# A first stage by half batches: ScalarE normalises, the gates go round by DMA in four rows, and VectorE adds the residual's bias

## The chip, the cores and the metric

One core of a Trainium2 chip runs the kernel. The metric is the device time of one execution in microseconds, the lower the better; the median of three runs is compared.

## The reference

One transformer block with modulation (adaLN), in float32, on x of 4 batches x 1024 tokens x 256:

```
mod = (silu(c) @ wmod)                  # 4 rows x 1536: sa, ca, ga, sb, cb, gb
ga, gb = sign(g) * max(|g|, 0.25)       # each gate is kept away from 0
h = layernorm(x) * (1 + ca) + sa
x = x + ga * attention(h)               # 8 heads, low-rank q, k, v (32 + 32 rotary columns), softmax
h = layernorm(x) * (1 + cb) + sb
x = x + gb * moe(h)                     # top 1 of 8 experts, capacity 768, exact gelu
```

`attention` ends in `o @ W_O + b_O`; the kernel carries the value path as 32 latent columns per head, so that W_UV and W_O fold into one matrix `proj` (256 x 256) and the biases into one row `attn_bias`.

## The kernel before

Four stages follow each other, each a block in which every engine runs its own written-out list; semaphores order them. All engines leave a block together. Here only stage one and the head of stage two matter.

**Stage one** (lines 185 to 518) makes for each batch b of 8 tiles (128 tokens each): the moments of x (`spread(b)`, VectorE, L312 to L317), the power -1/2 of the variance (GpSimd, L299), the normalised rows `xn` (VectorE, L324), their transposes (`turn(b)`, TensorE, L428), the modulated transposes `hT` (`features(b)`, ScalarE, L255, scale and shift from the columns `shiftT`), and with them two latents in PSUM: `latent(b, 0)` for the keys and `latent(b, 1)` for the queries (L443). ScalarE writes their high half (KA L265, KC L266, CQ L268), VectorE the low half (L403, L406) and KB (L408); `values(b)` turns KA (L452), and VectorE copies it to VV (L412). `latent(b + 1, ...)` waits on `lo_done` until the low half of batch b has been taken out of the same PSUM bank. `xn` and `hT` hold one batch.

Beside this TensorE does 15 `side` products in the one bank `t_ps2`, each of which waits until VectorE has copied the one before (`side_out`): 0 and 1 turn W_UQ, 2 turns W_UK and W_UV, 3 multiplies them (VectorE makes G and GQ of that, L339 to L350), 4 and 5 make `proj`, 6 makes `attn_bias`, and 7 to 14 make the four gates of each batch, replicated on all 128 partitions: the weights of that product are `silrep`, silu(c) spread over 128 columns, two products of 512 columns per batch (L489). VectorE copies each (L357) and after the second bounds the gates in five steps (L363 to L369) on 128 partitions. The columns `shiftT` come before all that from eight small products with `wm` as weights (L501).

The SP queue loads in this order: rows, x of batch 0, the first third of wmod, the up-weights (16 loads), x of batch 1, W_O, b_O, the rest of wmod, x of batches 2 and 3, and then writes zeros to the DRAM buffer `xbuf`, 6.4 MB; SP waits for those before it leaves the block. GpSimd fills constants, among them two of 4096 columns at 3.5 us each (L293), before its first power.

**Stage two** (from L520) runs the 32 heads. GpSimd starts it with `prepare(b)` for each batch (L733 to L741): `projb` = proj x gate, `gbias` = attn_bias x gate, and x1 += gbias over the batch's 2048 columns (L740). After that it makes `prob_lo` for most tiles (L745), and later normalises heads. TensorE first does queries (L652) and maxima (L633, L634), which VectorE reduces (L774), and scores from then on. `projb` and x1 are read only in stage three.

Of the kernel before, what the change touches and what calls it, by code (L numbers as in the profile page):

```python
# [41 lines left out]
def adaln_block(nc, h_t, W_DQ, b_DQ, W_UQ, b_UQ, W_DKV, b_DKV, W_UK, b_UK, W_UV, b_UV, W_QR, b_QR,  # L42
# [16 lines left out]
    out_rows = out.rearrange("b s d -> (b s) d")  # L59

    ctx = ExitStack()
    with ctx:
# [51 lines left out]

        one = ExitStack()
        xs = x1
# [13 lines left out]
        silrep = sb(one, "silrep", [P, B, KD, P])  # L130
        bvrep = sb(one, "bvrep", [P, H, P])
        onesrow = sb(one, "onesrow", [1, P])
        shiftT = sb(one, "shiftT", [P, 4, B])
# [4 lines left out]
        stats = sb(one, "stats", [P, ST, 6])  # L138
        mv = sb(one, "mv", [P, ST, 2])
        vare = sb(one, "vare", [P, ST])  # L140
        rstd = sb(one, "rstd", [P, ST])
        xn = sb(one, "xn", [P, ST, D])
        hT = sb(one, "hT", [P, KD, S])
        sign = sb(one, "sign", [P, 2, D])
        size = sb(one, "size", [P, 2, D])
# [6 lines left out]
        x_in = [sem(f"x_in{b}") for b in range(B)]  # L152
        rows_in = sem("rows_in")
        shift_in = sem("shift_in")
        up_in = sem("up_in")
        latent_in = sem("latent_in")
        gates_in = sem("gates_in")
# [5 lines left out]
        shift_ready = sem("shift_ready")  # L163
# [4 lines left out]
        gate_steps = sem("gate_steps")  # L168
        ln_v = sem("ln_v")
        ln_var = sem("ln_var")  # L170
        ln_rstd = sem("ln_rstd")
        ln_xn = sem("ln_xn")
# [6 lines left out]
        v_done = sem("v_done")  # L179

        SIDE = 7 + 2 * B

        with nc.Block() as block:
            @block.sync
            def _(sp):
# [4 lines left out]
                def load_x(b):  # L192
                    load(xs[:, b * ST:(b + 1) * ST, :], x_tiles[:, b * ST:(b + 1) * ST, :], x_in[b])
# [4 lines left out]
                wm_k = wmod.rearrange("(k p) n -> p k n", p=P)  # L198
                load(wm[:, :, 0:2 * D], wm_k[:, :, 0:2 * D], shift_in)
# [23 lines left out]
            def _(ac):  # L223
# [20 lines left out]
                def features(b):  # L244

                    if b == 0:
                        ac.wait_ge(shift_done, 2)
                    else:

                        ac.wait_ge(kq_ready, 2 * b)  # L250
                    for g in range(2):
                        for k in range(KD):
                            n = 4 * b + 2 * g + k
                            ac.wait_ge(xT_ready, n + 1)
                            nc.scalar.activation(hT[:, k, g * HALF:(g + 1) * HALF], t_ps[n % 2][:],  # L255
                                                 ACT.Identity, scale=shiftT[:, 2 + k, b:b + 1],
                                                 bias=shiftT[:, k, b:b + 1]).then_inc(hT_ready, 1)

                features(0)
                for b in range(B):  # L260

                    if b == 0:
                        ac.wait_ge(latent_in, 16 * 14)
                    ac.wait_ge(kq_ready, 2 * b + 1)
                    nc.scalar.activation(KA[:, b * S:(b + 1) * S], k_ps[:], ACT.Identity, bias=bk[:]).then_inc(hi_done, 1)  # L265
                    nc.scalar.activation(KC[LR:P, b, :], k_ps[LR:P, HALF:S], ACT.Identity, bias=bk[LR:P, :]).then_inc(hi_done, 1)  # L266
                    ac.wait_ge(kq_ready, 2 * b + 2)
                    nc.scalar.activation(CQ[0:3 * DC, b * S:(b + 1) * S], q_ps[0:3 * DC, :], ACT.Identity,  # L268
                                         bias=bq[:]).then_inc(hi_done, 1)
                    if b + 1 < B:  # L270
                        features(b + 1)

            @block.gpsimd
            def _(pool):
# [5 lines left out]
                for m in (ident, ident16):  # L280
# [8 lines left out]
                fills = ((ones16[:], 1.0), (onesrow[:], 1.0), (VV[:, :, 2 * DC:VP], 1.0),  # L289
                         (KB[LR:LR + 1, :], -1.0), (CQ[3 * DC:QROWS, :], 1.0))  # L290
                for n, (dst, value) in enumerate(fills):
                    pool.wait_ge(const_p, 9 + n)
                    nc.gpsimd.memset(dst, value).then_inc(const_p, 1)  # L293
                pool.wait_ge(const_p, 14)
                pool.wait_ge(const_v, 2)
                for b in range(B):

                    pool.wait_ge(ln_var, b + 1)
                    nc.gpsimd.tensor_tensor(rstd[:], vare[:], minus_half[:], ALU.pow).then_inc(ln_rstd, 1)  # L299

            @block.vector
            def _(v):
                nc.vector.memset(zeros[:], 0.0).then_inc(const_v, 1)
                nc.vector.memset(minus_half[:], -0.5).then_inc(const_v, 1)
# [3 lines left out]
                def spread(b):  # L308

                    v.wait_ge(x_in[b], 16)  # L310
                    for t in range(ST):
                        nc.vector.bn_stats(stats[:, t, :], xs[:, b * ST + t, :]).then_inc(ln_v, 1)  # L312
                    v.wait_ge(ln_v, b * (2 * ST) + ST)
                    for t in range(ST):
                        nc.vector.bn_aggr(mv[:, t, :], stats[:, t, :]).then_inc(ln_v, 1)
                    v.wait_ge(ln_v, (b + 1) * (2 * ST))
                    nc.vector.tensor_scalar(vare[:], mv[:, :, 1], EPS, None, ALU.add).then_inc(ln_var, 1)  # L317

                def normalise(b):
                    v.wait_ge(ln_rstd, b + 1)  # L320
                    if b:
                        v.wait_ge(xT_ready, 4 * b)
                    for t in range(ST):
                        nc.vector.tensor_scalar(xn[:, t, :], xs[:, b * ST + t, :], mv[:, t, 0:1],  # L324
                                                rstd[:, t:t + 1], ALU.subtract, ALU.mult).then_inc(ln_xn, 1)

                def side_out(n):
# [3 lines left out]
                    if n < 2:  # L331
                        nc.vector.tensor_copy(uqT[:, 4 * n:4 * n + 4, 0:QROWS],
                                              bank[:].rearrange("p (h c) -> p h c", h=4)[:, :, 0:QROWS]).then_inc(side_done, 1)
                    elif n == 2:
                        nc.vector.tensor_copy(ukvT[:], bank[:].rearrange("p (h c) -> p h c", h=H)).then_inc(side_done, 1)
                    elif n == 3:

# [6 lines left out]
                        v.wait_ge(side_done, 4)  # L344
# [6 lines left out]
                    elif n < 6:  # L351
                        nc.vector.tensor_copy(proj[:, n - 4, :], bank[:, 0:D]).then_inc(side_done, 1)
                    elif n == 6:
                        nc.vector.tensor_copy(attn_bias[:], bank[:, 0:D]).then_inc(side_done, 1)
                    else:
                        b, half = (n - 7) // 2, (n - 7) % 2
                        nc.vector.tensor_copy(mod[:, b, 2 * half:2 * half + 2, :],  # L357
                                              bank[:].rearrange("p (m d) -> p m d", m=2)).then_inc(side_done, 1)
                        if half:

                            v.wait_ge(side_done, n + 1)
                            g = mod[:, b, 0:4:3, :]
                            nc.vector.tensor_scalar(sign[:], g, 0.0, 2.0, ALU.is_ge, ALU.mult).then_inc(gate_steps, 1)  # L363
                            nc.vector.scalar_tensor_tensor(size[:], g, -1.0, g, ALU.mult, ALU.max).then_inc(gate_steps, 1)
                            v.wait_ge(gate_steps, 5 * b + 2)
                            nc.vector.tensor_scalar(g, size[:], 0.25, None, ALU.max).then_inc(gate_steps, 1)
                            v.wait_ge(gate_steps, 5 * b + 3)
                            nc.vector.scalar_tensor_tensor(g, sign[:], -1.0, g, ALU.add, ALU.mult).then_inc(gate_steps, 1)
                            nc.vector.tensor_scalar(mod[:, b, CB, :], mod[:, b, CB, :], 1.0, None, ALU.add).then_inc(gate_steps, 1)  # L369
                            v.wait_ge(gate_steps, 5 * b + 5)  # L370
# [5 lines left out]
                normalise(0)  # L376
                v.wait_ge(shift_ready, 1)
                nc.vector.tensor_copy(shiftT[:, 0:2, :], t_ps[1][:, 0:2 * B].rearrange("p (m b) -> p m b", b=B)).then_inc(shift_done, 1)
                nc.vector.tensor_scalar(shiftT[:, 2:4, :], t_ps[1][:, 2 * B:4 * B].rearrange("p (m b) -> p m b", b=B),
                                        1.0, None, ALU.add).then_inc(shift_done, 1)  # L380
                v.wait_ge(cols_done, 1)
                nc.vector.tensor_copy(bvrep[:], cols[:, 88:96].unsqueeze(2).broadcast_to([P, H, P])).then_inc(cols_done, 1)
                v.wait_ge(silu_done, 1)
# [1079 lines left out]
```

## Time and profile before

| what | value |
|---|---|
| median of 3 runs | 1013.93 us (1011.23 to 1013.94) |
| profiled execution | 1015.22 us, its span 1013.5 us |
| mean granted clock of TensorE | 0.940 |
| TensorE busy | 902.4 us, 89% |
| VectorE busy | 719.9 us, 71% |
| GpSimd busy | 679.5 us, 67% |
| ScalarE busy | 573.6 us, 57% |

The span runs from the first to the last instruction; the rest of the execution's time lies around it. Busy time counts instructions in the engine and not waiting. A line number is that of the kernel's file; the order of engines' work is what the lists above say.

### The profile page before, as it was taken

How to read it: one execution, taken by the hardware profiler on the slowest of the kernel's cores; microseconds unless marked ns; L12 is line 12 of the kernel's file. 1: busy time of each engine (PE TensorE's matmuls, PEld its weight loads, DVE VectorE, ACT ScalarE, POOL GpSimd, SP SyncE). 2: the span in 40 equal slices, each digit the busy share in tenths (PEclk: the TensorE clock that was granted, in tenths of full speed). 3: DMA queues.
4: the chain of work that ended last, by engine and by line, in shares of the span. 5: the costliest groups of instructions: out<-in, count | busy, mean ns of one | idle time of the engine just before them, and what ended most of it. 6: DMA issues, size and time to landing. Idle time of an engine off the chain costs nothing. (4 is left out here: it accounts for less than half of the span.)

```text
span 1013.5 us, 21524 instructions
## 1 busy us (share of the span) xinstructions
PE 902.4 (89%) x8438; PEld 540.9 (53%) x8438; DVE 719.9 (71%) x1344; ACT 573.6 (57%) x972; POOL 679.5 (67%) x445
## 2 busy tenths in 40 slices
PE   4896799999999999999999998973399999999995
PEld 3442144444444444445444446863167776777764
DVE  5677878888888888888988854873065676566643
ACT  1222367777777777777677672655175447544650
POOL 4102989999999999999999993598505434543452
PEclk9899599999999999999999997985599999999998
DMA  9700000000000000000000002458715334544110
GB/s 274 295 0 1 1 1 2 2 1 2 2 2 1 3 1 3 2 2 2 2 1 3 1 2 98 153 188 284 251 48 180 124 119 135 181 128 132 46 50 19
DMA packets 48222, 69.50 MB, mean 69 GB/s; under 512 B 7440, under 2 KB 40405, under 8 KB 48122
## 3 DMA queue, kind: packets, MB, share of 16 engines
q1 hardware_dynamic: 38170, 51.01, 15.1%
q0 software_dynamic: 7680, 16.87, 5.1%
q8 instruction: 68, 1.11, 0.5%
q10 hardware_dynamic: 2272, 0.24, 0.2%
q14 instruction: 32, 0.26, 0.1%
HBM read 44.66 MB, written 29.66 MB: 73 GB/s over the span
## 5 line engine op out<-in xcount | busy, mean ns | idle before, releaser
L745 POOL TENSOR_TENSOR prob_lo<-prob 128x1024 f16<-128x1024 f32 x208 | 437.2, 2132 | 36.2 <-ACT prob L700 36.2
L700 ACT ACTIVATE prob<-st_ps 128x512 f32<-128x512 f32 x512 | 301.8, 597 | 134.8 <-PE st_ps L624 132.4
L774 DVE TENSOR_REDUCE part_max<-x_ps 128x1 f32<-128x512 f32 x512 | 325.1, 678 | 69.9 <-PE x_ps L634 68.9
L623 PE MATMUL st_ps<-QA,KA 128*128 128x512 f16 x512 | 199.3, 389 | 0.5 <-ACT prob L700 0.5
L624 PE MATMUL st_ps<-QB,KB 65*128 65x512 f16 x512 | 197.9, 387 | 0.0
L672 PE MATMUL acc_ps<-VV,prob 128*128 128x65 f16 x2048 | 159.6, 194 | 4.3 <-POOL prob_lo L745 4.3
L672 PEld LDWEIGHTS acc_ps<-VV,prob 128*128 128x128 bf16 x2048 | 143.9, 98 | 34.1 <-POOL prob_lo L745 6.8
L672 PE MATMUL acc_ps<-VV,prob_lo 128*128 128x65 f16 x2048 | 158.9, 194 | 0.0
L672 PEld LDWEIGHTS acc_ps<-VV,prob_lo 128*128 128x128 f16 x2048 | 135.2, 98 | 30.2 <-issue 0.5
L1255 POOL DMA_INDIRECT out<-yo,xb x48 | 47.7, 994 | 154.0 <-DVE yo L1362 149.1
L633 PE MATMUL x_ps<-KA,QA 64*128 64x512 f16 x256 | 102.9, 402 | 20.7 <-DVE part_max L774 20.7
L1285 ACT ACTIVATE act_f<-g_ps,cols 128x768 f32<-128x768 f32 x64 | 57.7, 901 | 105.0 <-PE g_ps L1408 98.2
L1333 DVE TENSOR_TENSOR act_l<-act_f,act_h 128x768 f16<-128x768 f32 x64 | 59.9, 956 | 72.7 <-ACT act_h L1293 71.7
L1423 PE MATMUL y_ps<-w2h,act_h 128*128 128x256 f16 x384 | 104.8, 273 | 4.2 <-DVE act_l L1333 4.2
L1423 PE MATMUL y_ps<-w2h,act_l 128*128 128x256 f16 x384 | 104.7, 273 | 0.0
L1423 PE MATMUL y_ps<-w2l,act_h 128*128 128x256 f16 x384 | 104.7, 273 | 0.0
L634 PE MATMUL x_ps<-KC,QA 64*128 64x512 f16 x256 | 102.8, 402 | 0.0
L633 PEld LDWEIGHTS x_ps<-KA,QA 64*128 64x128 f16 x256 | 23.8, 93 | 123.3 <-DVE part_max L774 120.2
L623 PEld LDWEIGHTS st_ps<-QA,KA 128*128 128x128 f16 x512 | 49.7, 97 | 60.4 <-issue 37.1
L1248 POOL DMA_INDIRECT tb<-tbuf,xb x48 | 63.9, 1332 | 17.0 <-issue 14.3
L791 DVE TENSOR_TENSOR prob_lo<-prob 128x1024 f16<-128x1024 f32 x48 | 61.1, 1274 | 6.2 <-ACT prob L700 6.2
L1408 PE MATMUL g_ps<-xh,w1h 128*128 128x384 f16 x256 | 53.4, 332 | 1.8 <-DVE xl L1327 1.4
(176 smaller groups left out, 1391.0 us busy)
## 6 DMA issues: line engine op xcount, KB each, us to landing
w1f<-in_L_ffn_w SPq DMA_DIRECT2D x8, 1024.0 KB, 4.9
w2f<-in_L_ffn_w SPq DMA_DIRECT2D x8, 1024.0 KB
xbuf<-zeros SPq DMA_DIRECT2D x7, 910.0 KB, 14.0
xb<-xbuf SPq DMA_DIRECT2D x8, 780.0 KB
x<-in_L_attn_h_t SPq DMA_DIRECT2D x4, 1024.0 KB, 10.3
out<-x SPq DMA_DIRECT2D x4, 1024.0 KB
tbuf<-x SPq DMA_DIRECT2D x4, 1024.0 KB
tbuf<-gb_row SPq DMA_DIRECT2D x4, 1024.0 KB
```

What stands on the lines that cost most here:

```text
L623: mm(st_ps[i % 2][:], KA[:, at], QA[:, n % QRING, half], start=True, stop=False)
L624: mm(st_ps[i % 2][:], KB[:, at], QB[:, n % QRING, half], start=False, stop=True).then_inc(scores_ready, 1)
L633: mm(x_ps[i % 3][:], QA[0:LR, n % QRING, at], KA[0:LR, b * S:b * S + HALF], start=True, stop=True)
L634: mm(x_ps[(i + 1) % 3][:], QA[LR:P, n % QRING, at], KC[LR:P, b, :], start=True, stop=True).then_inc(smax_ready, 1)
L672: last = mm(acc_ps[:, q, 0:VC], part[:, k, q * P:(q + 1) * P], VV[:, b * ST + k, 0:VC], start=k == 0 and q % 4 == 0 and i == 0, stop=k == ...
L700: nc.scalar.activation(prob[:, k, f * HALF:(f + 1) * HALF], st_ps[i % 2][:], ACT.Exp).then_inc(exp_done, 1)
L745: nc.gpsimd.tensor_tensor(prob_lo[:, k, :], prob[:, k, :], prob_top[:, k, :], ALU.subtract).then_inc(sub_pool, 1)
L774: nc.vector.tensor_reduce(part_max[:, n % 2, item // 2, item % 2:item % 2 + 1], x_ps[i % 3][:], AX.X, ALU.max).then_inc(smax_done, 1)
L791: nc.vector.tensor_tensor(prob_lo[:, k, :], prob[:, k, :], prob_top[:, k, :], ALU.subtract).then_inc(sub_vector, 1)
L1248: nc.gpsimd.indirect_dma_start(out=tb[:, s, :], out_offset=None, in_=tbuf, in_offset=bass.IndirectOffsetOnAxis(ap=who(e, s), axis=0), boun ...
L1333: V.tensor_tensor(act_l[:, f, :], act_f[:, i % 3, :], act_h[:, f, :], ALU.subtract).then_inc(act_low, 1)
L1423: last = mm(y_ps[s % 2][:, 0:D], x[:, f, s * P:(s + 1) * P], w[:, u, f, :], start=c == 0 and f == 0, stop=c == 2 and f == FT - 1)
```

## The change

Stage one is rearranged, by groups of four tiles (half a batch):

- Loads, moments, powers, normalising, turning and features go by group; x comes in eight loads, and all of wmod before the second of them. `xn` holds four groups and `hT` two batches.
- `xn` is made by ScalarE as rstd * x + nmr, with a new column nmr = -mean * rstd made by VectorE (`shift_of`).
- The gates are made for the four batches on four partitions: three products of 4 x 512 (`side` 0, 2, 3), bounded once (`bound_gates`), stored to DRAM (`kept_gates`, 16 KB) and loaded to all 128 partitions in one DMA (2 MB). The shift columns are four small transposes of the first product (`side` 1). `silrep` goes. Both DMAs and SP's waits for them stand before the zeros.
- `prepare` goes from GpSimd in stage two to VectorE in stage one, spread over the end of its list.
- Each engine's list is a new order; the first two powers stand between GpSimd's constants.

The core of the diff (declarations, unchanged bodies and the renumbering of `side` left out):

```diff
@@ sync
-                load(wm[:, :, 0:2 * D], wm_k[:, :, 0:2 * D], shift_in)
+                load(wm[:], wmod.rearrange("(k p) n -> p k n", p=P), mod_w_in)
+                load_x(1)
...
-                load_x(1)
+                load_x(2)
+                load_x(3)
                 load(wo[:], W_O.rearrange("(h d) n -> d h n", d=DK), wo_in)
                 load(bo[:], b_O.rearrange("(a n) -> a n", a=1), wo_in)
-                load(wm[:, :, 2 * D:6 * D], wm_k[:, :, 2 * D:6 * D], gates_in)
-                load_x(2)
-                load_x(3)
+                for g in range(4, NG):
+                    load_x(g)
+                sp.wait_ge(gate_steps, GATE_STEPS)
+                sp.dma_start(kept_gates, gate_row[:].rearrange("b m d -> b (m d)")).then_inc(gates_kept, 16)
+                sp.wait_ge(gates_kept, 16)
+                sp.dma_start(mod[:].rearrange("p b m d -> p (b m d)"),
+                             kept_gates.rearrange("(a b) n -> a (b n)", a=1).broadcast_to([P, B * 4 * D])).then_inc(mod_in, 16)
@@ scalar
+                def normalise(g):
+                    ac.wait_ge(ln_shift, g + 1)
+                    if g >= 4:
+                        ac.wait_ge(xT_ready, 2 * (g - 4) + 2)
+                    for t in range(GROUP):
+                        n = GROUP * g + t
+                        nc.scalar.activation(xn[:, g % 4, t, :], xs[:, n, :], ACT.Identity, scale=rstd[:, n:n + 1],
+                                             bias=nmr[:, n:n + 1]).then_inc(ln_xn, 1)
+                normalise(0)
+                normalise(1)
                 features(0)
+                features(1)
+                normalise(2)
                 for b in range(B):
                     (KA and KC of b)
+                    if b + 1 < B:
+                        features(2 * b + 2)
+                        normalise(2 * b + 3)
+                    if b + 2 < B:
+                        normalise(2 * b + 4)
                     (CQ of b)
                     if b + 1 < B:
-                        features(b + 1)
+                        features(2 * b + 3)
@@ gpsimd, stage one
+                power(0)
+                fill(12, KB[LR:LR + 1, :], -1.0)
+                power(1)
+                fill(13, CQ[3 * DC:QROWS, :], 1.0)
+                for g in range(2, NG):
+                    power(g)
@@ vector
-                        nc.vector.tensor_scalar(xn[:, t, :], xs[:, b * ST + t, :], mv[:, t, 0:1],
-                                                rstd[:, t:t + 1], ALU.subtract, ALU.mult).then_inc(ln_xn, 1)
+                def shift_of(g):
+                    at = slice(g * GROUP, (g + 1) * GROUP)
+                    v.wait_ge(ln_rstd, g + 1)
+                    nc.vector.scalar_tensor_tensor(nmr[:, at], mv[:, at, 0], -1.0, rstd[:, at], ALU.mult, ALU.mult).then_inc(ln_shift, 1)
+                def prepare(b):
+                    if b == 0:
+                        v.wait_ge(mod_in, 16)
+                        v.wait_ge(side_done, BIAS + 1)
+                    (the three operations that GpSimd had: projb, gbias, x1 += gbias)
                 spread(0)
-                (normalise, shift columns, bvrep, silrep; then per batch: side_outs, spread, normalise, low halves, values)
+                shift_of(0); spread(1); side_out(SHIFT); shift_of(1); side_out(COLUMNS)
+                spread(2); side_out(GATES); side_out(GATES + 1); bound_gates(); shift_of(2)
+                spread(3); side_out(UQ); shift_of(3); side_out(UQ + 1); side_out(UKV); spread(4)
+                (bvrep); keys_low(0); shift_of(4); spread(5); queries_low(0); shift_of(5); take_values(0); spread(6)
+                (constants); shift_of(6); keys_low(1); spread(7); side_out(PROJ); side_out(PROJ + 1); shift_of(7)
+                queries_low(1); take_values(1); side_out(BIAS); keys_low(2); prepare(0); queries_low(2)
+                side_out(GQS); take_values(2); prepare(1); keys_low(3); prepare(2); queries_low(3)
+                take_values(3); prepare(3)
@@ tensor
-                            last = mm(bank[:], silrep[:, b, k, :], wm[:, k, (2 + 2 * half) * D:(4 + 2 * half) * D],
-                                      start=k == 0, stop=k == KD - 1)
+                            last = mm(bank[0:B, :], silc[:, :, k], wm[:, k, c * HALF:(c + 1) * HALF], start=k == 0, stop=k == KD - 1)
+                side(SHIFT); turn(0); side(COLUMNS); side(GATES); turn(1); side(GATES + 1); side(UQ)
+                latent(0, 0); side(UQ + 1); turn(2); side(UKV); latent(0, 1); turn(3); values(0)
+                latent(1, 0); turn(4); side(PROJ); latent(1, 1); side(PROJ + 1); turn(5); values(1)
+                side(BIAS); latent(2, 0); turn(6); latent(2, 1); side(GQS); turn(7); values(2)
+                latent(3, 0); latent(3, 1); values(3)
@@ gpsimd, stage two
-                for b in range(B):
-                    prepare(b)
```

## Rows read from the trace of the kernel before

**Rows 1.** The page, its head.

```profile
span 1013.5 us, 21524 instructions
```

**Rows 2.** Windows: us, busy us of PE, PEld, DVE, ACT, POOL, clock, DMA share, GB/s.

```profile
0.00:95.00 95.00, 72.02 (x275) 39.05 (x275) 63.28 (x172) 24.91 (x30) 15.93 (x22) 0.96 0.46 152
```

**Rows 3.** Timeline where stage one meets two: start, us, engine, line, what [idle before].

```profile
94.50 0.49 DVE L412 COPY VV<-v_ps 128x256 f16<-128x256 f16 x2
...
95.29 1.27 POOL L734 TENSOR_TENSOR projb<-proj,mod 128x512 f32<-128x512 f32 x1 [24.10 <-POOLq L185]
95.31 0.38 PE L652 MATMUL side_ps<-CQ,GQ 98*128 98x512 f16 x1 [1.98 <-PEq L185]
...
121.21 9.30 POOL L745 TENSOR_TENSOR prob_lo<-prob 128x1024 f16<-128x1024 f32 x5
```

**Rows 4.** Groups of VectorE in stage one: count, busy us, mean ns, idle before.

```profile
L312 DVE BATCH_NORM_STATS2 stats<-x 128x6 f32<-128x256 f32 x32 | 10.8, 412 | 3.7 <-DMA x<-in_L_attn_h_t 3.7
L324 DVE TENSOR_SCALAR xn<-x,mv,rstd 128x256 f32<-128x256 f32 x32 | 10.7, 406 | 1.9 <-POOL rstd L299 1.9
L357 DVE COPY mod<-t_ps 128x512 f32<-128x512 f32 x8 | 5.5, 691 | 7.8 <-PE t_ps L489 7.8
L403 DVE SCALAR_TENSOR_TENSOR KA<-k_ps,bk,KA 64x1024 f16<-64x1024 f32 x4 | 5.2, 1291 | 0.1
L406 DVE SCALAR_TENSOR_TENSOR CQ<-q_ps,bq,CQ 32x1024 f16<-32x1024 f32 x4 | 5.1, 1276 | 0.2
...
L368 DVE SCALAR_TENSOR_TENSOR mod<-sign,mod 128x512 f32<-128x512 f32 x4 | 2.8, 692 | 0.1
...
L408 DVE COPY KB<-KA 64x1024 f16<-64x1024 f16 x4 | 1.7, 420 | 0.1
```

**Rows 5.** Timeline of VectorE, batch 0: G and GQ (six operations), then low keys.

```profile
33.22 0.42 DVE L339 TENSOR_SCALAR G<-t_ps 98x256 f32<-98x256 f32 x1 [1.66 <-PE t_ps L477]
...
37.11 1.29 DVE L403 SCALAR_TENSOR_TENSOR KA<-k_ps,bk,KA 64x1024 f16<-64x1024 f32 x1
```

**Rows 6.** TensorE: gate products as a group, then the bias and a latent in the timeline.

```profile
L489 PE MATMUL t_ps<-wm,silrep 128*128 128x512 f32 x32 | 15.4, 602 | 1.6 <-DVE mod L357 1.6
...
47.57 3.62 PE L484 MATMUL t_ps<-wo,bvrep 128*128 128x256 f32 x16
51.12 0.69 PE L485 MATMUL t_ps<-bo,onesrow 1*128 1x256 f32 x2
...
69.80 3.60 PE L443 MATMUL q_ps<-hT,wq 128*96 128x512 f32 x8
```

**Rows 7.** Groups of GpSimd: the wide addition in stage two, powers in stage three.

```profile
L740 POOL TENSOR_TENSOR x<-x,gbias 128x2048 f32<-128x2048 f32 x4 | 18.0, 4498 | 0.3
...
L981 POOL TENSOR_TENSOR rstd<-var,minus_half 128x4 f32<-128x4 f32 x8 | 8.2, 1031 | 20.0 <-DVE var L1030 20.0
```

**Rows 8.** Groups of VectorE in stage three: its only two-input shape of 2048 columns.

```profile
L1105 DVE TENSOR_TENSOR w1l<-w1f,w1h 128x2048 f16<-128x2048 f32 x1 | 2.3, 2293 | 5.0 <-issue 5.0
```

**Rows 9.** Groups of ScalarE in stage one.

```profile
L255 ACT ACTIVATE hT<-t_ps,shiftT 128x512 f32<-128x512 f32 x16 | 11.8, 774 | 10.9 <-PE t_ps L428 10.4
L265 ACT ACTIVATE KA<-k_ps,bk 128x1024 f16<-128x1024 f32 x4 | 4.5, 1114 | 32.9 <-PE k_ps L443 32.9
...
L266 ACT ACTIVATE KC<-k_ps,bk 64x512 f16<-64x512 f32 x4 | 2.7, 682 | 0.1
```

**Rows 10.** Windows for the loads, the standstill and the clock; columns as in rows 2.

```profile
0.00:18.00 18.00, 5.70 (x25) 5.24 (x25) 9.66 (x36) 2.00 (x3) 10.99 (x19) 1.00 0.92 235
...
36.00:38.40 2.40, 0.00 (x0) 0.00 (x0) 2.33 (x3) 0.78 (x2) 0.00 (x0) 1.00 1.02 416
39.30:46.10 6.80, 5.67 (x21) 2.05 (x14) 5.48 (x23) 0.00 (x0) 0.00 (x0) 0.50 0.66 269
97.70:117.40 19.70, 10.68 (x33) 1.95 (x32) 17.92 (x30) 3.83 (x6) 19.46 (x10) 0.50 0.00 0
117.40:131.60 14.20, 14.20 (x62) 4.44 (x61) 8.36 (x14) 7.45 (x14) 13.11 (x6) 0.51 0.00 1
```

More of the change, by code:

```diff
@@ L113, in adaln_block @@
         mrow = sb(inner, "mrow", [ST, 2, P], fp16)
+        latents = ExitStack()
+        projb = latents.enter_context(nc.sbuf_tensor("projb", [P, B, KD, D], fp32, side="right"))
         one = ExitStack()
+        GROUP = 4
+        NG = NT // GROUP
         xs = x1
@@ L242, in _, with features @@
                                      ACT.Silu).then_inc(silu_done, 1)
[L244 to L257, printed above, removed]
+                def normalise(g):
[6 more added lines that the diff above has]
+                                             bias=nmr[:, n:n + 1]).then_inc(ln_xn, 1)
+                def features(g):
+                    b, half = g // 2, g % 2
+                    if g == 0:
+                        ac.wait_ge(shift_done, 1)
+                        ac.wait_ge(side_done, COLUMNS + 1)
+                    if b >= 2:
+                        ac.wait_ge(kq_ready, 2 * (b - 1))
+                    for k in range(KD):
+                        ac.wait_ge(xT_ready, 2 * g + k + 1)
+                        nc.scalar.activation(hT[:, b % 2, k, half * HALF:(half + 1) * HALF], t_ps[k][:],
+                                             ACT.Identity, scale=shiftT[:, 2 + k, b:b + 1],
+                                             bias=shiftT[:, k, b:b + 1]).then_inc(hT_ready, 1)
+                normalise(0)
+                normalise(1)
                 features(0)
+                features(1)
+                normalise(2)
                 for b in range(B):
@@ L287, in _, with fill @@
                 nc.gpsimd.iota(iota_i[:, 2 * E:2 * E + 1], pattern=[[0, 1]], base=SLOTS, channel_multiplier=1).then_inc(const_p, 1)
[L289 to L292, printed above, removed]
+                def fill(n, dst, value):
+                    pool.wait_ge(const_p, n)
@@ L301, in _ @@
             @block.vector
             def _(v):
+                nc.vector.memset(minus_half[:], -0.5).then_inc(const_v, 1)
                 nc.vector.memset(zeros[:], 0.0).then_inc(const_v, 1)
-                nc.vector.memset(minus_half[:], -0.5).then_inc(const_v, 1)
                 v.wait_ge(const_v, 2)
                 nc.vector.memset(zeros[:].bitcast(i32)[:, :, D:D + 1], NOBODY).then_inc(const_v, 1)
[L308 to L317, printed above, removed]
@@ new lines, in take_values @@
+                def take_values(b):
+                    v.wait_ge(v_ready, b + 1)
+                    for low in range(2):
+                        nc.vector.tensor_copy(VV[:, b * ST:(b + 1) * ST, (1 - low) * DC:(2 - low) * DC],
+                                              v_ps[:, :, low * LR:low * LR + DC]).then_inc(v_done, 1)
+                def prepare(b):
+                    if b == 0:
+                        v.wait_ge(mod_in, 16)
+                        v.wait_ge(side_done, BIAS + 1)
+                    nc.vector.tensor_tensor(projb[:, b, :, :], proj[:],
+                                            mod[:, b, GA, :].unsqueeze(1).broadcast_to([P, KD, D]), ALU.mult).then_inc(scaled, 1)
+                    if b:
+                        v.wait_ge(biased, b)
+                    nc.vector.tensor_tensor(gbias[:], attn_bias[:], mod[:, b, GA, :], ALU.mult).then_inc(gbias_done, 1)
+                    v.wait_ge(gbias_done, b + 1)
+                    v.wait_ge(ln_xn, (b + 1) * ST)
+                    nc.vector.tensor_tensor(x1[:, b * ST:(b + 1) * ST, :], x1[:, b * ST:(b + 1) * ST, :],
+                                            gbias[:].unsqueeze(1).broadcast_to([P, ST, D]), ALU.add).then_inc(biased, 1)
@@ L375, in _ @@
                 spread(0)
[L376 to L380, printed above, removed]
+                shift_of(0)
+                spread(1)
+                side_out(SHIFT)
+                shift_of(1)
+                side_out(COLUMNS)
+                spread(2)
+                side_out(GATES)
+                side_out(GATES + 1)
+                bound_gates()
+                shift_of(2)
+                spread(3)
+                side_out(UQ)
+                shift_of(3)
+                side_out(UQ + 1)
+                side_out(UKV)
+                spread(4)
                 v.wait_ge(cols_done, 1)
                 nc.vector.tensor_copy(bvrep[:], cols[:, 88:96].unsqueeze(2).broadcast_to([P, H, P])).then_inc(cols_done, 1)
[L383 to L384 removed]
+                keys_low(0)
+                shift_of(4)
+                spread(5)
+                queries_low(0)
+                shift_of(5)
+                take_values(0)
+                spread(6)
                 v.wait_ge(const_p, 9)
@@ L496, in _ @@
                 te.wait_ge(silu_done, 1)
-                te.wait_ge(shift_in, 16)
-                for m in range(4):
-                    for k in range(KD):
-                        last = mm(t_ps[1][:, m * B:(m + 1) * B], wm[:, k, m * P:(m + 1) * P], silc[:, :, k],
-                                  start=k == 0, stop=k == KD - 1)
-                last.then_inc(shift_ready, 1)
-                te.wait_ge(shift_done, 2)
-                for b in range(B):
-                    turn(b)
-                    if b:
-                        values(b - 1)
-                    side(4 * b)
-                    side(4 * b + 1)
-                    latent(b, 0)
-                    side(4 * b + 2)
-                    latent(b, 1)
-                    if 4 * b + 3 < SIDE:
-                        side(4 * b + 3)
-                values(B - 1)
+                te.wait_ge(mod_w_in, 16)
+                side(SHIFT)
+                turn(0)
+                side(COLUMNS)
+                side(GATES)
+                turn(1)
+                side(GATES + 1)
+                side(UQ)
+                latent(0, 0)
+                side(UQ + 1)
+                turn(2)
+                side(UKV)
+                latent(0, 1)
+                turn(3)
+                values(0)
+                latent(1, 0)
+                turn(4)
+                side(PROJ)
+                latent(1, 1)
+                side(PROJ + 1)
+                turn(5)
+                values(1)
+                side(BIAS)
+                latent(2, 0)
+                turn(6)
+                latent(2, 1)
+                side(GQS)
+                turn(7)
+                values(2)
+                latent(3, 0)
+                latent(3, 1)
+                values(3)
         one.close()
         two = inner
-        latents = ExitStack()
-        projb = latents.enter_context(nc.sbuf_tensor("projb", [P, B, KD, D], fp32, side="right"))
         o_n = latents.enter_context(nc.sbuf_tensor("o_n", [P, NT, D], fp32, side="right"))
```

253 lines of the change are left out of this document (136 added, 117 removed).

## The prediction, made before the changed kernel was run

> **What bounds the kernel now.** I read first how the span divides. The profiled execution took 1015.22 us for a span of 1013.5 [rows 1]. The diff changes the first stage, which fills the first 95 us, and takes one piece of work off GpSimd at the head of the second. So the question is how long the first stage becomes. The window over it [rows 2] shows TensorE busy 72.0 us, VectorE 63.3, ScalarE 24.9, GpSimd 15.9: no engine is full, and the stage is bound by hand-overs between TensorE and VectorE. It ends with VectorE's last copy at 94.5 to 95.0, and TensorE and GpSimd start the second stage at 95.3 [rows 3].
>
> The grouped instructions of VectorE [rows 4] show what stands between the hand-overs: the normalising of x (L324, 10.7 us), eight copies of gates (5.5), and the bounding of gates, which is done for every batch on all partitions. How far VectorE is behind can be seen in the first batch: it makes G and GQ from 33.2, comes to KA's low half only at 37.1 [rows 5], and TensorE, which turns KA after that, stands still from 36.0 to 38.4 [rows 10].
>
> GpSimd starts the second stage with `prepare`, 95.3 to 121.2, 6.5 us for each of four batches (4.5 of it the wide addition [rows 7]), and only then subtracts for the first time [rows 3]. The last window of [rows 10] shows that this delays nothing: from 117.4 to 131.6 TensorE is busy 14.20 of 14.20 us, at half clock. The exponentials and products are paced by TensorE there, not by `prob_lo`. Before that the pace is VectorE's (17.92 of 19.7 us busy, reducing maxima).
>
> **What leaves.** TensorE loses 15.4 us of gate products (L489) [rows 6] and gains three products of 512 columns in four rows: 15.4/8 = 1.9 us each, 5.7 in all, since the rows that come out don't change the columns that go through. VectorE loses L324 (10.7), eight copies (5.5) and the four batches of gate arithmetic, of whose five steps the last product alone is 2.8 (about 10 with the rest, by the widths). It gains three copies of 0.69 and one round of that arithmetic (2.5). GpSimd's 26 us of `prepare` go, and are worth nothing by themselves, because TensorE covers them as shown. Without that cover, the exposed part would be the 3 us from the exponentials of the first tile to 121.2.
>
> **What VectorE takes on.** `prepare` on VectorE isn't in the trace. The nearest rows are two-input operations of its own: 0.692 us for 512 columns [rows 4] and 2.293 for 2048 [rows 8]; 256 columns lie on the same line at 0.42. So a batch costs 0.69+0.42+2.29 = 3.4, with starts 3.5. The upper end is GpSimd's own 6.5 [rows 3]; I take 3.5, because row and engine are the same. Below nothing it can't go.
>
> **The normalising on ScalarE.** From 512 to 1024 columns ScalarE's price rises from 682 to 1114 ns, 0.216 us for 256 columns. An operation with scale and bias in columns takes 774 for 512, so 558 for 256 [rows 9]. Back to back I take 0.54 per tile, 2.2 per group of four, 17.3 in all. ScalarE then has about 42 us of work, far from full, but each group stands in its queue between copies that others wait for. Ends: 0.41, VectorE's price in L324 [rows 4], and 0.774; over the two groups on the path that is -1 to +2 us.
> The Trainium skill (ScalarE: Activation LUTs, What ACT_TABLE_LOAD costs) says that each per-partition pointer operand adds about 93 ns, an element 0.833 ns, and that neighbours overlap by 93 ns; an estimate by it is 0.49 a tile. The sum would then be 0.4 us less. No row here shows two operands on 256 columns.
>
> **The sum, as a chain through the new order** (latent products 3.5 per call of eight records [rows 6], turning a group about 1.0, low keys 1.29+0.42, low queries 1.28, spread of four tiles 4x0.34+0.37+0.17 = 1.9 from [rows 4] and the moments behind it; about 0.03 to 0.1 for a hand-over):
> 1. x arrives in half batches. Ahead of group 2 stand x groups 0 and 1 (1.0 MB), all of wmod (1.5), the up-weights (0.9), group 2 (0.5) and the small loads (0.3): 4.2 MB. At 235 GB/s over the first 18 us [rows 10] that is 18.0 us. The first two groups and wmod don't decide, if they are there by 14.
> 2. 18.0 to 28.2: spread 1.9, first gate copy 0.7, second gate product 2.0, its copy 0.7, turning of uq 0.65, keys' latents 3.7, and ScalarE still 0.5 in group 2.
> 3. 28.2 to 41.2: KA and KC 1.8, features 1.5, normalising 2.2, then 2.6 of waiting for VectorE, which spreads group 4, fills bvrep and takes low keys (to 36.4); normalising 2.2, CQ 1.1, features 1.5. TensorE stands still for 3.3 us here, from 38.
> 4. 41.2 to 49.3: half the keys' latents 1.85, KA and KC 1.8, low keys 1.75, spread 1.9, the copy of proj 0.5 and its hand-over.
> 5. 49.3 to 59.5: second half of proj 0.75, turning 1.0, values 0.6, bias 4.2 (47.57 to 51.8 in [rows 6]), keys' latents 3.5, hand-over.
> 6. 59.5 to 61.4: KA and KC.
> 7. 61.4 to 86.3: from here VectorE has no gap. Two low keys 3.4, two low queries 2.6, G and GQ 3.9 [rows 5], two times values 1.0, four `prepare` 14.0. TensorE ends near 77.
>
> So the stage ends at 86.3 and not at 95.0: 8.7 us less. `prepare` is 14 us of the unbroken stretch at the end, and much of what was taken from VectorE is given back there. The second stage then starts after TensorE has idled some 9 us, at half clock: its first two products take 0.6 in place of 0.38, 0.4 us lost [rows 3]. Net 8.3: a span of 1005.2, 1006.9 for an execution like the profiled one, which lay 1.3 above the median; against the median 1013.93 I forecast 1005.6.
>
> **The gates' round trip.** The rows are final at about 26 us. The store waits behind the last x groups (some 28), and the 2 MB spread to all partitions take 5 at the 416 GB/s of [rows 10]: there by about 38, needed at 63. The 6.4 MB of zeros follow it on SP's queue and take 16 us more, to 54; the stage's end, which waits for them, has 30 us to spare.
>
> **Rivals.** *The clock falls in the new gap* (0.27). Before, a standstill of 2.4 us was followed by 6.8 us at half clock [rows 10]; the new one from 38 to 41 is longer. Seven us at half from there cost 1.8 to 2.5 us in steps 4 and 5, fourteen cost 6: 1007.5 to 1011.5.
> *The clock stays low* (0.05, the slower side): the sparse stretch at 97.7 to 131.6 stayed at half for 34 us. If the gap at 38 brings that and the latents of all later batches run at half, 20 us cost 7.7 and 25 us cost 12.4, and the kernel is slower than before from about 22 us on: 1014 to 1018.
> *The gates arrive late* (0.04): the spread reads one row 128 times and could be far slower than contiguous loads. Each us beyond 63 lengthens the stage by one; from 72 on nothing is gained, and the zeros behind it would then hold the end too.
> *The freed GpSimd or an earlier full clock pays in the second stage* (0.14): if the clock comes back 3 to 6 us earlier than at 131.6, half of that is gained, on top of a chain that is a little faster: 1001 to 1003.
> *The new queues only move the stall* (0.10): four engines in a fixed order, with GpSimd's powers (1.03 each [rows 7]) between two steps of VectorE in every half batch; a slip of 0.3 at each of the eight and an x that comes 3 us late would leave 3 us or less: 1011 to 1014.
> The forecast as it stands, 1003.5 to 1007.5, has 0.40.
>
> **Range and chances.** 0.3% is 3.0 us, about what three runs of this kernel can tell from nothing; faster means below 1010.9. All of the forecast and of the second-stage case, and most of the first rival, lie there: 0.83. Within: 0.11. Slower: 0.06. The range 1001.5 to 1011.5 leaves out the low clock, the late gates and half of the moved stall above, and little below.
>
> **What would show it.** In the profile after: the last instruction of the first stage (VectorE's wide addition) at 86 and not 95; VectorE without a gap from 61, the wide addition at 2.29 us; the ScalarE tile at 0.55; no gate transfer waited for; the granted clock between 38 and 50; GpSimd's first subtraction right behind the exponentials, with TensorE's pace at that place unchanged. Wrong would be: VectorE waiting in its last 25 us, half clock over the latents, or a later stage that moved.

## The result and the profile after

The changed kernel takes 1003.18 us, the median of five runs (1002.41 to 1006.59), against 1013.93 before: a ratio of 0.9906, interval 0.9885 to 0.9928. The same kernel, run again beside other experiments, gave 1005.08 and 0.9916 [0.9895, 0.9937]. Of the eleven runs together the median is 1004.5. The profiled execution took 1002.61 us.

The page's head and busy times, to set beside [rows 1]:

```profile
span 1000.9 us, 21467 instructions
PE 881.8 (88%) x8406; PEld 527.7 (53%) x8406; DVE 713.9 (71%) x1315; ACT 588.0 (59%) x1004; POOL 655.7 (66%) x437
```

The junction of the stages in the timeline, which answers to [rows 3]: VectorE's last unbroken stretch (its start and its end), TensorE's first instruction of stage two, and GpSimd's first subtraction (that of `prob_lo`, the low half of the exponentials).

```profile
61.19 1.29 DVE L425 SCALAR_TENSOR_TENSOR KA<-k_ps,bk,KA 64x1024 f16<-64x1024 f32 x1 [5.06 <-ACT KC L297]
...
62.85 0.68 DVE L445 TENSOR_TENSOR projb<-proj,mod 128x512 f32<-128x512 f32 x1
63.46 0.41 DVE L449 TENSOR_TENSOR gbias<-attn_bias,mod 128x256 f32<-128x256 f32 x1
63.90 2.29 DVE L452 TENSOR_TENSOR x<-x,gbias 128x2048 f32<-128x2048 f32 x1
...
83.38 2.29 DVE L452 TENSOR_TENSOR x<-x,gbias 128x2048 f32<-128x2048 f32 x1
85.99 0.59 PE L751 MATMUL side_ps<-CQ,GQ 98*128 98x512 f16 x1 [8.29 <-PEq L199]
109.36 1.89 POOL L834 TENSOR_TENSOR prob_lo<-prob 128x1024 f16<-128x1024 f32 x1 [59.36 <-ACT prob L799]
```

The span is 12.6 us shorter. Stage two starts 9.3 earlier (95.31 to 85.99), so 3.3 more are won behind it. The windows over its head, with the columns of [rows 10], say where:

```profile
86.00:106.30 20.30, 9.87 (x30) 1.83 (x31) 16.68 (x28) 3.94 (x6) 0.00 (x0) 0.50 0.00 1
106.30:114.50 8.20, 8.20 (x22) 1.89 (x20) 5.67 (x9) 4.14 (x8) 3.79 (x2) 0.50 0.00 0
114.50:120.00 5.50, 5.48 (x55) 2.28 (x53) 4.44 (x8) 4.12 (x8) 5.44 (x3) 1.00 0.01 3
```

TensorE is full from 106.3 on, still at half clock, for 8.2 us; before it was so for 14.2 [rows 10]. Six us less at half the rate are 3.0 us of work. The experiments show below that this is the execution's and not the change's. GpSimd, idle through the first of these windows, waits for the exponentials when it comes to its first subtraction.

### The profile page after: what moved, and what is told of

Read it like the earlier page. It is cut to its first block and busy times, and to the rows that moved or that the text cites. A ratio compares the mean times of both kernels' runs of the same rounds, so it can differ in the third digit from the quotient of the medians.

```text
span 1000.9 us, 21467 instructions
## 1 busy us (share of the span) xinstructions
PE 881.8 (88%) x8406; PEld 527.7 (53%) x8406; DVE 713.9 (71%) x1315; ACT 588.0 (59%) x1004; POOL 655.7 (66%) x437
```

## The experiments

Two numbers divide every run below: where stage two starts (TensorE's first product there) and where GpSimd writes the first head's output. I call the stretch between them the head. What follows the output takes 864 to 866 us in all of them.

| kernel | median us | ratio to before | stage two starts | head | span |
|---|---|---|---|---|---|
| before | 1013.93 | | 95.3 | 52.6 | 1013.5 |
| after | 1003.18 | 0.9906 | 86.0 | 49.6 | 1000.9 |
| after, again | 1005.08 | 0.9916 | 84.9 | 52.6 | 1003.1 |
| gates alone | 1005.00 | 0.9922 | 85.1 | 50.3 | 1001.0 |
| prepare back on GpSimd | 993.34 | 0.9812 | 75.3 | 51.1 | 990.1 |
| the same, again | 992.97 | 0.9804 | 75.1 | 49.1 | 989.9 |
| GpSimd kept busy | 1004.11 | 0.9915 | 85.5 | 52.0 | 1002.5 |
| VectorE normalises | 1015.38 | 1.0020 | 98.7 | 49.2 | 1011.8 |
| VectorE normalises, fills first | 1010.63 | 0.9966 | 92.0 | 52.0 | 1008.6 |
| prepare split | 993.83 | 0.9813 | 76.4 | 51.0 | 991.4 |
| GpSimd prepares, TensorE fed | 991.67 | 0.9792 | 75.1 | 49.1 | 988.9 |
| the same, again | 992.22 | 0.9786 | 76.3 | 49.1 | 991.2 |
| prepare split, TensorE fed | 987.54 | 0.9740 | 77.0 | 44.7 | 987.2 |

The span and what is read from a trace belong to one execution of each, the medians to 5 to 12 runs in five rounds. "Before" beside them had medians of 1013.54 to 1013.71. The expectations call the runs by number: e1 is `prepare` back on GpSimd, e2 GpSimd kept busy, e3 VectorE normalises, e4 the gates alone, e5 the fills first, e6 TensorE fed, e7 `prepare` split, e8 split and fed. The runs stood on several chips, so a difference of a few us between two medians is surest where the ratios differ by more than their intervals.

The column of heads shows how far executions differ: 49.6 and 52.6 for one kernel, 51.1 and 49.1 for another. Where TensorE is not fed (see below), they are 49.1 to 52.6 with `prepare` on GpSimd at the start of stage two, and 49.2 to 52.6 without it. So a difference of 3 us between two heads is no evidence by itself, and nothing here shows that a GpSimd that is free shortens the head.

**`prepare` back on GpSimd**, all else as in the change:

```diff
@@ vector
-                prepare(0)
...
-                prepare(3)
@@ gpsimd, stage two
+                for b in range(B):
+                    prepare(b)
```

> The changed kernel with prepare put back on GpSimd at the head of stage two. Theory (prepare on VectorE is 14 us of an unbroken stretch that sets the end of stage one, and on GpSimd it was covered): stage one ends at 76 to 78 instead of 85.7, GpSimd prepares until about 103, some 3 us behind the first exponentials, and TensorE isn't held by it: 993 to 996 us. Rival (the free GpSimd is what let the second stage run 3 us shorter than before): the stage end is the same 77, but the second stage is 3 us longer again: 997 to 999 us. Rival (VectorE's end is not the bound, TensorE's is): 1000 or more.

993.34 us, 0.9812 [0.9785, 0.984]; repeated, 992.97. The timeline:

```profile
74.44 0.49 DVE L439 COPY VV<-v_ps 128x256 f16<-128x256 f16 x2
75.23 1.26 POOL L819 TENSOR_TENSOR projb<-proj,mod 128x512 f32<-128x512 f32 x1 [26.50 <-POOLq L200]
...
96.68 4.50 POOL L825 TENSOR_TENSOR x<-x,gbias 128x2048 f32<-128x2048 f32 x1
101.14 3.74 POOL L830 TENSOR_TENSOR prob_lo<-prob 128x1024 f16<-128x1024 f32 x2
```

Stage two starts 10.7 us earlier, or 9.7 against the execution of the changed kernel whose clock did not fall in stage one either (84.9). The medians differ by 9.8 and, in the repetitions, by 12.1. So moving `prepare` to VectorE costs this kernel 10 to 12 us, of the 14 that it puts into VectorE's last unbroken stretch. GpSimd comes to its first subtraction 4.9 us after the first exponential starts (96.22), where a GpSimd that is free comes 2.2 us after it (107.18 and 109.36 in the changed kernel); at half clock that costs nothing that the medians show.

**GpSimd kept busy** at the head of stage two by additions into `o_n`, which is overwritten later, to see if its freedom gave the 3 us:

```diff
@@ gpsimd, stage two
+                for b in range(B):
+                    (o_n of the batch = x1 + x1, 8 tiles, then 3 tiles)
```

> The changed kernel with extra additions on GpSimd at the head of stage two, about 26 us of them in the shapes of the old prepare, written to a buffer that is overwritten later. Theory (the 3 us won in the second stage come from TensorE's clock, which returned to full 28 us after the stage's start instead of 36, and that has nothing to do with GpSimd): same as the changed kernel within 0.2%, 1001.5 to 1005.5. Rival (the free GpSimd gives them): the first subtraction comes 26 us into the stage and the time is 3 us longer, 1005.5 to 1007.5, with the clock back some 36 us into the stage.

1004.11 us, beside 1005.08 and 1003.18 without them: nothing. They were shorter than meant, 5.1 us a batch in place of 6.5, and ended at 106.3, where `prepare` would end near 111.4; but GpSimd's next instruction then waited 2.6 us for ScalarE. So up to 106 us a busy GpSimd costs nothing. That the full 25.9 us cost nothing either is what the heads with `prepare` on GpSimd show (49.1 to 52.6).

**VectorE normalises**, as before the change but in the new order:

```diff
@@ vector
-                    nc.vector.scalar_tensor_tensor(nmr[:, at], mv[:, at, 0], -1.0, rstd[:, at], ALU.mult, ALU.mult)
+                    for n in range(GROUP * g, GROUP * (g + 1)):
+                        nc.vector.tensor_scalar(xn[:, g % 4, n % GROUP, :], xs[:, n, :], mv[:, n, 0:1],
+                                                rstd[:, n:n + 1], ALU.subtract, ALU.mult).then_inc(ln_xn, 1)
```

> The changed kernel with xn made by VectorE again, in the places where it made the nmr column, and nothing of it on ScalarE. Theory (VectorE's list sets the end; the tiles cost it 0.33 each and sit partly in its gaps): stage one ends at 87 to 90, the time is 1 to 4 us above the changed kernel, 1004.5 to 1007. Rival (all 10.7 us land on VectorE's path): 1013. Rival (ScalarE's queue, where the tiles stand between copies, costs as much as VectorE gains): 1001 to 1003.5.

1015.38 us, no faster than before, 10 to 12 slower than the change. The theory's range missed, and the rival's size was nearer. The timeline of VectorE and GpSimd:

```profile
9.79 4.64 DVE L372 TENSOR_SCALAR xn<-x,mv,rstd 128x256 f32<-128x256 f32 x4 [1.26 <-POOL rstd L326]
9.81 3.50 POOL L321 MEMSET KB<- 1x4096 f16 x1
...
17.56 3.68 DVE L372 TENSOR_SCALAR xn<-x,mv,rstd 128x256 f32<-128x256 f32 x1 [0.62 <-POOL rstd L326]
17.58 3.51 POOL L321 MEMSET CQ<- 2x4096 f16 x1
```

A tile of 0.41 us takes 3.68, the length of the fill that GpSimd starts beside it; so does one of the four at 9.79. That is 6.5 us at the very place where the chain begins. Not every operation is held: in the changed kernel four tiles of moments start at 18.07, inside the fill from 16.03 to 19.54, and take their usual 1.41 us. Besides that VectorE has 10.7 us more to do [rows 4], less 1.3 for the `nmr` columns, and the granted clock fell twice in the stage (0.76 and 0.77 over 36 to 50 and 50 to 64).

The Trainium skill (SBUF — State Buffer, Who interferes with whom) says that a VectorE instruction in a mode that uses two ports and a GpSimd instruction exclude each other for the whole length of the one that came first. The length agrees here: 3.68 beside 3.50. Who came first can't be read from these rows, in which the tile's record starts 0.02 us ahead of the fill's, and no run here shows the mode.

**The fills first**, the same with the two fills ahead of the first power:

```diff
@@ gpsimd, stage one
-                power(0)
                 fill(12, KB[LR:LR + 1, :], -1.0)
-                power(1)
                 fill(13, CQ[3 * DC:QROWS, :], 1.0)
-                for g in range(2, NG):
+                for g in range(NG):
```

> The kernel of e3 (VectorE makes xn) with GpSimd's two fills of 4096 columns put ahead of its first power, where the kernel before had them. In e3 two of VectorE's tiles took 3.68 us in place of 0.41, both starting within 0.02 us of one of those fills (3.50 us), and TensorE was 5 to 7 us late from there. Theory (the tile waits for the fill, and that with what follows is most of the 12 us that e3 lost): no tile above 0.45 us, stage one ends at 88 to 91 and not 98, 1005 to 1008 us. Rival (the coincidence is none, VectorE's load is the loss): 1011 to 1015.

1010.63 us, above the 1005 to 1008 of the theory and just under the rival's range. Four tiles take 1.38 us, none of them stands still, and the fills explain 4.8 us. The rest, 5.6 us over the changed kernel on the same chip, goes with VectorE's longer list and with a clock of 0.76 over 50 to 64 and 0.82 over 64 to 92; the two were not separated. The stall also found another victim, the operation on four columns ahead of the first power (0.17 us elsewhere). It starts inside the fill and ends with it, at 10.57 beside 10.54:

```profile
7.03 3.51 POOL L321 MEMSET CQ<- 2x4096 f16 x1
8.28 2.29 DVE L356 TENSOR_SCALAR vare<-mv 128x4 f32<-128x4 f32 x1
```

**The gates alone**: the kernel before with its order, its loads and its `prepare` on GpSimd, but gates on four rows (without `silrep`) and the round trip by DMA, here behind the zeros on SP's queue:

```diff
-                            nc.vector.tensor_copy(mod[:, b, 2 * half:2 * half + 2, :], bank...)
+                        nc.vector.tensor_copy(gate_row[:, 2 * half:2 * half + 2, :], bank[0:B, :]...)
@@ sync
+                (store gate_row to kept_gates, load it to all partitions as mod)
```

> The kernel before with one part of the change: the gates made once on four rows and sent round by DMA; prepare stays on GpSimd. It takes 11.6 us of products from TensorE and about 12 us from VectorE. Theory (in the kernel before, the gate products and their copies stand in the hand-overs of the last two batches, so most of the change's gain in stage one is this part): stage one ends at 84 to 87, 1003 to 1006 us. Rival (they filled waits): 1010 or more.

1005.00 us, 0.9922 [0.9895, 0.9949]: 8.7 us, by itself as much as the whole change by its second comparison (8.6) and most of it by the first (10.8).

**The changed kernel again**, to size the spread between executions:

> The changed kernel unaltered, as the reference of this group on one chip. 1001.5 to 1006.5 us; the runs with a higher mean granted clock are the shorter ones.

1005.08 us, and the runs with the higher clock were indeed the shorter ones (1002.04 at 0.945, 1007.23 at 0.936). In the profiled execution the clock did not fall at the gap near 38 us, and the stage ended 1.1 us earlier. But it came back later in stage two, so that the span was 2.2 us longer. The windows:

```profile
38.00:48.00 10.00, 7.03 (x28) 3.00 (x28) 7.86 (x29) 7.88 (x13) 1.90 (x3) 1.00 1.01 420
85.00:105.00 20.00, 9.58 (x29) 1.64 (x28) 16.59 (x27) 3.94 (x6) 0.00 (x0) 0.50 0.00 1
105.00:120.00 15.00, 15.00 (x54) 4.11 (x52) 9.11 (x16) 7.32 (x13) 9.00 (x5) 0.50 0.00 1
```

Fifteen us full at half clock stand against 8.2 in the other execution, with the same instructions. The 3.0 us that the first profile showed in the head are thus no property of the change.

**TensorE fed.** `prepare` on GpSimd, and products that nobody reads in the gaps of TensorE: three at the end of stage one, behind a wait for VectorE's last copy of a side product, and two or three at each step of the first queries and maxima.

```diff
@@ tensor, stage two
+                def spin(count):
+                    for n in range(count):
+                        mm(acc_ps..., KA[:, 0:P], KA[:, 0:HALF], start=True, stop=True)
...
+                            if p < -1 or (p == -1 and k < 4):
+                                spin(2)
```

> The kernel of e1 (prepare on GpSimd) with products on TensorE that nobody reads, to keep it active: three at the end of stage one and two or three behind each query and pair of maxima until the scores begin. Theory (the half clock at the head of stage two costs time only where TensorE is the pace, from the first scores to the clock's return, some 10 us of which half is lost): the clock stays at full and 4 to 6 us are won, 987 to 990 us. Rival (GpSimd, 3 us behind the exponentials at half clock, becomes the pace at full clock): 990 to 992. Rival (the products themselves hold the maxima up, as each pair has 1.37 us of VectorE to hide in): 994 or more.

991.67 us; repeated, 992.22: 0.8 to 1.7 under the kernel without them, where I expected 4 to 6, and inside the intervals, so that a gain of the products alone is not shown. The clock stays whole while they run, and then TensorE is early: it waits for GpSimd, and the clock falls there. Its windows:

```profile
75.50:90.00 14.50, 10.54 (x45) 2.48 (x43) 12.72 (x22) 2.39 (x4) 14.33 (x8) 1.00 0.00 0
90.00:102.00 12.00, 10.36 (x45) 2.63 (x45) 11.50 (x21) 8.17 (x14) 11.86 (x5) 1.00 0.01 2
102.00:108.00 6.00, 5.03 (x45) 2.32 (x46) 1.88 (x4) 1.93 (x4) 6.00 (x4) 0.72 0.01 2
```

and its timeline, GpSimd's last `prepare`, its first subtraction right behind, and the product that waits for it:

```profile
96.55 4.51 POOL L837 TENSOR_TENSOR x<-x,gbias 128x2048 f32<-128x2048 f32 x1
101.02 5.59 POOL L842 TENSOR_TENSOR prob_lo<-prob 128x1024 f16<-128x1024 f32 x3
...
102.97 0.20 PE L763 MATMUL acc_ps<-VV,prob 128*128 128x65 f16 x1 [1.69 <-POOL prob_lo L842]
```

**`prepare` split**: batch 0's on VectorE, in the gap of 5.06 us that stands in the timeline after at 61.19; the others on GpSimd.

```diff
+        POOL_FROM = 1
@@ vector
                 side_out(BIAS)
+                prepare(0)
                 keys_low(2)
@@ gpsimd, stage two
+                for b in range(POOL_FROM, B):
+                    prepare(b)
```

> The kernel of e1, but batch 0's prepare stays on VectorE and moves into the 5 us in which it waits ahead of the third batch's low keys; GpSimd does the other three. Theory (that gap is free, and GpSimd's late start isn't on the path either): the end of stage one and the time are those of e1, 991.5 to 995.5, and the first subtraction comes right behind the exponentials. Rival (GpSimd's start matters): 1 to 3 us less, 989 to 992. Rival (VectorE's gap is not free): 995 to 997.

993.83 us, equal to all four on GpSimd (993.34, 992.97). At half clock a GpSimd that is free 6.5 us sooner is worth nothing that these runs can tell. VectorE's gap is free: the wait for ScalarE behind `prepare(0)` shrinks from 5.06 to 1.60 us. Stage two starts 1.2 us later than in e1, but VectorE copies `attn_bias` 1.2 us later too, ahead of the moved work; in this execution the clock fell near 40 us, and in e1's it did not.

**Both**, split and fed:

> e7 and e6 together: batch 0's prepare in VectorE's gap, the other three on GpSimd, and the unread products on TensorE. In e6 the clock stayed at full until 103, and then the first value products waited 1.7 us for GpSimd, whose first subtraction came at 101.0. Theory (with full clock GpSimd's late start is the pace; three batches of 6.5 us end it by 95 to 96, ahead of the first exponentials): no such wait, and 1.5 to 3 us less than e6 on the same chip. Rival (GpSimd has no slack over the first heads and gives the gain back): within 1 us of e6.

987.54 us, 0.974 [0.972, 0.976], beside 992.22 for the one that is only fed: 4.7 us, more than the 1.5 to 3 that I expected, and clear of the spread (986.2 to 989.0 against 990.7 to 993.5). The windows:

```profile
75.50:90.00 14.50, 11.20 (x45) 2.69 (x43) 11.89 (x21) 2.39 (x4) 12.88 (x7) 1.00 0.00 0
90.00:102.00 12.00, 10.08 (x45) 2.63 (x45) 11.50 (x21) 6.75 (x12) 10.74 (x6) 1.00 0.00 0
102.00:108.00 6.00, 6.00 (x71) 2.84 (x69) 5.20 (x10) 4.08 (x9) 5.31 (x4) 1.00 0.02 4
```

Now GpSimd's first subtraction starts at 97.65, 3.4 us sooner, TensorE is full from 102 on, and the clock doesn't fall in the head, which is 44.7 us. Of the 4.5 us by which it is shorter than in e6, my estimate puts 1.7 to the wait that is gone and 1.7 to the half clock behind it (some 3.4 us at half rate between 102 and 108 in e6); the rest is not traced. This is the best version, 26 us under before and some 16 to 18 under the change. The two run again beside it, for scale:

> e1 unaltered, as a reference of this group on one chip: 991 to 996 us.

> e6 unaltered, as the other reference of this group: 990 to 994 us, and 1 to 3 us less than e1.

They took 992.97 and 992.22 us. The second is 0.8 under the first and not 1 to 3.

## Why the prediction was right, step by step

**The forecast of 1005.6** lies 2.4 above the first median, 0.5 above the second and 1.1 above that of all eleven runs. The first median is just outside the narrow forecast of 1003.5 to 1007.5, and just above the 1001 to 1003 of the rival with a shorter second stage. The chances were added up wrongly: 0.40 and 0.14 and all of the first rival's 0.27 make 0.81, and I wrote 0.83 for "faster".

**The chain of steps 1 to 7** came out in the order foretold. x group 2 is read at 18.07 (18.0), ScalarE starts on the keys of batch 0 (KA, its high half) at 27.83 (28.2), the second half of batch 1's keys at 39.93 (41.2), the wait for low keys of batch 2 ends at 61.19 (61.4). From there VectorE has no gap, and four `prepare` take 0.68+0.41+2.29 us each, as taken from its other operations. TensorE ends at 77.7 (77). The stage ends at 85.7, not 86.3. Three of these points in the timeline after, with ScalarE's tiles:

```profile
18.07 1.41 DVE L361 BATCH_NORM_STATS2 stats<-x 128x6 f32<-128x256 f32 x4 [1.37 <-DMA x<-in_L_attn_h_t]
...
39.93 3.42 PE L536 MATMUL k_ps<-hT,wk 128*128 128x512 f32 x4 [2.56 <-ACT hT L282]
...
46.58 4.04 ACT L270 ACTIVATE xn<-x,nmr,rstd 128x256 f32<-128x256 f32 x8
```

**ScalarE's tile** was priced a little high: eight back to back take 4.04 us, 0.505 each, where I had 0.54; four in a group take 2.07. The estimate of 0.49 by the Trainium skill (ScalarE: Activation LUTs, What ACT_TABLE_LOAD costs) was nearer.

**"The clock falls in the new gap"** had 0.27. It happened in one of the two profiled executions of the change, and in four of the seven others whose kernels have the same first half of stage one (e2, e7, e8 and the second of e6), so it was about even. What was mis-sized is its price. In the first execution TensorE stood for 2.56 us, and the clock was half for some 3.3 us:

```profile
39.00:42.00 3.00, 2.07 (x3) 1.04 (x4) 2.90 (x9) 0.88 (x2) 0.00 (x0) 0.57 1.00 417
42.00:45.00 3.00, 3.00 (x20) 1.56 (x19) 0.83 (x9) 1.58 (x2) 1.01 (x1) 0.86 1.00 417
```

At half rate that is 1.7 us, under the 1.8 to 2.5 of the rival's lower case, which assumed 7 us at half. The chain was 1.3 us ahead by then and 0.2 ahead at 61.19. Without the fall the stage ended at 84.6, 1.1 us earlier.

**"GpSimd's 26 us are worth nothing by themselves"** held: kept busy, it cost nothing, and freed by 6.5 us at half clock, it gave nothing. It ceases to hold when TensorE runs at full clock there, which is the condition that the prediction named in other words ("Without that cover"): freeing 6.5 of the 26 us is then worth 4.7 us, where the prediction had 3 for all of them.

**"Much of what was taken from VectorE is given back there"** held, at 10 to 12 of the 14 us. I saw this cost, took it into the sum, and did not ask whether the move was worth making: the prediction says itself that GpSimd's 26 us were covered. The change is the sum of about -8.7 for the gates (measured on the kernel before), about -12 for half batches, new loads and ScalarE's normalising (993.3 against 1005.0), and +10 to +12 for the moved `prepare`. The second term was not split further on a kernel with the old order. With VectorE normalising in the new order all of the gain was gone, of which 4.8 us was the collision with the fills.

**The step that was mis-sized** is the start of stage two. I took its head to be unchanged but for 0.4 us. It was 3.0 shorter in one execution and equal (52.6) in the other. The first profile is thus a lucky one for the change, and a forecast of one median can be no better than such a spread. What differed between them was how long the half clock outlasted the thin stretch. The rival "an earlier full clock" thus describes single executions, not the kernel; its other half, the freed GpSimd, finds no support in the heads of the table. Why the clock returns 28.5 us after the start in one and 35 in the other is open.

**The gates' round trip** ended when foretold, at 37.6 (forecast 38), but partly by luck. The rows were final at 25.7 and the store went out at once, at 25.77, and not behind the x loads at 28; it took 2.9 us. The spread was issued at 28.92 and took 8.7 us, where I had 5 at 416 GB/s; the zeros were issued right behind it, from 29.30. SP's wait for the store in the chain of its own queue:

```profile
SPq L233 <- DMA kept_gates<-gate_row: 2.9, 1, 2.9
```

## What to carry to other kernels

Before work is moved from one engine to another, ask whether it was covered where it stood: `prepare` cost nothing on GpSimd, because TensorE at half clock was the pace, and cost 10 to 12 us on VectorE, which closed the stage alone. Put such work into a gap that the trace shows (here 5 us before 61) rather than at the end of a full list. A value needed on all partitions, but computed alike on each, is cheaper on a few rows with a DMA to spread it, when it has tens of us to travel.

## What the runs showed of the hardware

- VectorE's TENSOR_SCALAR on SBUF stood still until a GpSimd fill beside it had ended: 3.68 us in place of 0.41, and 2.29 in place of 0.17 for four columns. The fills write one and two partitions. The moments (BATCH_NORM_STATS2) ran at their usual 1.41 us for four tiles beside such a fill.
- After a stretch in which TensorE was busy 9.9 of 20.3 us, at half clock, the clock stayed at half for 8.2 us after the engine was full again in one execution, and after 9.6 of 20.0 us for 15.0 us in another of the same kernel. With the gaps filled by products that nobody reads the clock stayed full until TensorE had to wait for GpSimd, which was the next to set the pace; a gain of that alone is not shown (0.8 to 1.7 us, inside the intervals). With GpSimd relieved as well it stayed full through the whole head.
- One and the same order of TensorE, with a standstill of some 2.6 us near 38, brought a fall of the clock in five of nine profiled executions and none in the other four. In the two pairs of one kernel the fall moved the start of stage two by 1.1 and 1.2 us.
